# A recommender tower on one core: layer 2 and the MLP one chunk later in TensorE's order of work

## The reference, cut to what matters

```python
# B = 1024 samples, 39 fields, 16 dims; three cross layers of 128 channels each, then an MLP
e = stack([tbl_f[ids[:, f]] for f in range(39)], axis=1)          # 1024 x 39 x 16
xk = e
for W in (f0, f1, f2):                                            # (39*39|128*39|128*39) x 128
    z = einsum('bfd,bgd->bfgd', e, xk).reshape(b, f * g, d)
    xk = einsum('bpd,pm->bmd', z, W);  outs.append(xk)
z = sum(concatenate(outs, axis=1), axis=-1)                       # 1024 x 384
h = concatenate([z, dense_ctx], axis=1)                           # 1024 x 400
h = maximum(h @ W_top1 + b_top1, 0)                               # 512
h = maximum(h @ W_top2 + b_top2, 0)                               # 256
y = h @ W_top3                                                    # 1
```

## Time and profile before

| | |
|---|---|
| median of 3 runs | 1388.26 us (1387.1 to 1389.87) |
| the profiled execution | 1386.06 us |
| its span in the trace | 1383.9 us |
| TensorE busy | 1308.5 us, 95% |
| VectorE, ScalarE, GpSimd busy | 81%, 65%, 51% |
| mean granted TensorE clock | 0.996 |

### The profile page before, as it was taken

How to read it: one execution, slowest core, us unless ns; L and a number is a source line. 1 busy time by engine, 2 the same in 40 slices (tenths; PEclk the granted TensorE clock), 3 DMA queues, 4 the chain that set the end, 5 groups by cost and what they waited for, 6 DMA issues and landing times.

```text
span 1383.9 us, 20103 instructions
## 1 busy us (share of the span) xinstructions
PE 1308.5 (95%) x5912; PEld 997.4 (72%) x5912; DVE 1126.5 (81%) x2794; ACT 905.7 (65%) x3233; POOL 705.0 (51%) x698
## 2 busy tenths in 40 slices
PE   1399999999999999999999999999999999999998
PEld 0356776777777777777777777777777777777787
DVE  2068988888888888888888888888888888888885
ACT  2046776766767676677767667676766777676664
POOL 7786556654545556454566545455564532333200
PEclk9989999999999999999999999999999999999999
DMA  5171021100311012110211003110121102110000
GB/s 138 27 224 47 17 71 50 50 27 3 95 30 43 27 38 68 49 30 14 70 50 50 27 4 95 30 43 28 37 69 50 30 12 68 47 47 26 1 2 0
DMA packets 51172, 63.51 MB, mean 46 GB/s; under 512 B 13067, under 2 KB 24344, under 8 KB 51019
## 3 DMA queue, kind: packets, MB, share of 16 engines
q1 hardware_dynamic: 34544, 56.08, 13.1%
q0 software_dynamic: 10128, 2.98, 2.0%
q10 hardware_dynamic: 6392, 3.18, 0.9%
HBM read 11.08 MB, written 1.02 MB: 9 GB/s over the span
## 4 chain that ended last, share of the span: by engine, by line
PE 77%; DVE 10%; ACT 6%; POOL 3%; issue 3%; DMA 1%; ACTq 0%; DVEq 0%
PE Y L763 17%; PE Y L765 16%; PE Y L764 16%; PE C L711 14%; PE C L725 5%; ACT Y L486 5%; PE S L719 4%; POOL rows L347 3%; DVE sum_a L635 2%; DVE sum_a L630 2%; DVE sum_b L630 2%; DVE z L599 1%; PE C L743 1%; PE S L685 1%; DVE cur L655 1%
## 5 line engine op out<-in xcount | busy, mean ns | idle before, releaser
L486 ACT ACTIVATE Y<-Y,x_col 128x128 f32<-128x128 f32 x2944 | 799.1, 356 | 392.6 <-PE Y L765 379.0
L763 PE MATMUL Y<-f_high,cur_high 128*128 128x512 f32 (+1 forms) x1280 | 626.1, 489 | 10.3 <-DVE part L643 5.0
L764 PE MATMUL Y<-f_low,cur_high 128*128 128x512 f32 (+1 forms) x1280 | 496.2, 388 | 0.0
L765 PE MATMUL Y<-f_high,cur_low 128*128 128x512 f32 (+1 forms) x1280 | 495.9, 387 | 0.0
L385 POOL TENSOR_TENSOR pairs<-shifted,base 117x512 f32<-117x512 f32 x186 | 240.0, 1292 | 462.2 <-PE C L711 460.2
L347 POOL DMA_INDIRECT rows<-in_tbl_dram,ids_sb x312 | 306.8, 983 | 76.8 <-issue 62.9
L763 PEld LDWEIGHTS Y<-f_high,cur_high 128*128 128x128 f32 x1280 | 241.6, 189 | 121.9 <-issue 45.1
L764 PEld LDWEIGHTS Y<-f_low,cur_high 128*128 128x128 f32 x1280 | 242.4, 189 | 89.8 <-issue 52.2
L765 PEld LDWEIGHTS Y<-f_high,cur_low 128*128 128x128 f32 x1280 | 240.9, 188 | 48.6
L630 DVE SCALAR_TENSOR_TENSOR sum_b<-Y,x_col,sum_b 128x128 f32<-128x128 f32 x768 | 262.5, 342 | 0.0
L711 PE MATMUL C<-pairs,f_sum 117*128 117x512 f32 (+1 forms) x448 | 231.5, 599 | 5.2 <-DVE pairs L593 5.2
(11 more groups left out here) (83 smaller groups left out, 660.1 us busy)
## 6 DMA issues: line engine op xcount, KB each, us to landing
shifted<-x_seq SPq DMA_DIRECT2D x157, 234.0 KB
base<-x_seq SPq DMA_DIRECT2D x95, 78.0 KB
rows<-in_tbl_dram,ids_sb POOLq DMA_INDIRECT x312
shifted<-x_seq SPq DMA_DIRECT2D x31, 156.0 KB
G<-in_L_rec_f_dram ACTq DMA_DIRECT2D x3, 832.0 KB, 11.8
w_sb<-in_W_top_dram SPq DMA_DIRECT2D x1, 768.0 KB
f_ext<-in_L_rec_f_dram SPq DMA_DIRECT2D x1, 760.5 KB
w_sb<-in_W_top_dram SPq DMA_DIRECT2D x1, 512.0 KB
```

Source lines behind the costliest of these rows:

```text
L486: ins = act.activation(where[:, i * M:(i + 1) * M], where[:, i * M:(i + 1) * M], ACT.Copy, scale=x_col[:, t // JT % QG, t % JT, f:f + 1])
L763: pe.matmul(where, ch, wh, start=True, stop=False)
L764: pe.matmul(where, ch, wl, start=False, stop=False)
L765: pe.matmul(where, cl, wh, start=False, stop=True).then_inc(y_filled, 1)
```

## The change

Layer 2's four portions are issued at slots 1 to 4 and no longer at 0 to 3 (`AT_L2 = 1`), with the waits that belong to them. The MLP's first layer is issued ahead of chunks 1 and 2 and no longer 0 and 1 (`AT_MLP1 = 1`); its second stays ahead of chunk 5; its last stands ahead of chunk 0 of the next tile and no longer ahead of chunk 9 (`AT_MLP3 = CH`). The chunks, and the programs of the other engines, keep their order.

```diff
 L2_SLICES = [range(0, 4), range(4, 7), range(7, 10), range(10, 13)]
+AT_L2 = 1
+AT_MLP1, AT_MLP2, AT_MLP3 = 1, 5, CH
...
-                    if q and bt and s < len(L2_SLICES):
-                        if s == 0:
+                    if q and bt and AT_L2 <= s < AT_L2 + len(L2_SLICES):
+                        if s == AT_L2:
                             pe.wait_ge(s_read, S_BEFORE["G", TPB * bt - 1] + 1)
                             pe.wait_ge(c_read, C_USE["l2", bt - 1, q - 1])
-                        layer2(bt - 1, [L2_F * (q - 1) + f for f in L2_SLICES[s]], L2_F * (q - 1), L2_F * q)
-                    if mlp is not None and j == mlp_tile(g):
-                        if c == 0:
-                            pe.wait_ge(c_read, C_USE["mlp", mlp, 0])
-                        if c < 2:
-                            mlp1(mlp, (2 * c, 2 * c + 1))
-                        if c == 5:
-                            pe.wait_ge(c_read, C_USE["mlp", mlp, 1])
-                            mlp2(mlp)
-                        if c == 9:
-                            pe.wait_ge(c_read, C_USE["mlp", mlp, 2])
-                            mlp3(mlp)
+                        layer2(bt - 1, [L2_F * (q - 1) + f for f in L2_SLICES[s - AT_L2]], L2_F * (q - 1), L2_F * q)
+                    stage = s - CH * mlp_tile(g) if mlp is not None else None
+                    if stage == AT_MLP1:
+                        pe.wait_ge(c_read, C_USE["mlp", mlp, 0])
+                        mlp1(mlp, (0, 1))
+                    if stage == AT_MLP1 + 1:
+                        mlp1(mlp, (2, 3))
+                    if stage == AT_MLP2:
+                        pe.wait_ge(c_read, C_USE["mlp", mlp, 1])
+                        mlp2(mlp)
+                    if stage == AT_MLP3:
+                        pe.wait_ge(c_read, C_USE["mlp", mlp, 2])
+                        mlp3(mlp)
```

## The result

| | before | after |
|---|---|---|
| median | 1388.42 us (1387.1 to 1389.87, 6 runs) | 1409.85 us (1409.19 to 1411.58, 6 runs) |
| ratio, 95% interval | | 1.0157 (1.0147 to 1.0168) |
| span of the profiled execution | 1383.9 us | 1407.8 us |
| chunk 0 of group 1 to the first matmul of the last chunk | 1242.31 us | 1265.12 us |

The change costs 21.4 us. The exception is group 7, whose last tile was up to 1.4 us longer in some executions (0.2 to 0.6 in four others); where this bears on a reading, the text says so.

The account below looks back on a forecast made before the run. TensorE's stream, busy 95% of the span, was taken as the bound. Uncovered chunk 0 costs 29.6 us, less 2.7 and 1.4 for the MLP's waits: +25.5 us on 1388.26, so 1413.8 us, range 1407 to 1421.

Parts of the forecast that it names:

- the first term: Chunk 0 without cover in 27 groups: 21 starts 1.13 us later and six 0.98 us later, 29.6 us in all.
- Just in time: Group 9 before the change: L643 ended at 436.46 and chunk 0 started at 436.51, read as no delay.
- The second count: Same loss counted from chunk 0 on: 0.10 us later plus 0.93 for four fields behind, 27 x 1.03 = 27.8 us.
- The MLP's first layer: Chunk 0 uncovered in six groups with the MLP in tile 0: 1.13 us later each.
- The MLP's second layer: L743's wait for relu1 on ScalarE goes in seven tiles: 0.38 us each, 2.7 us gained; bounds nothing to 2.7.
- The MLP's last layer: L749's wait for relu2 goes in seven tiles, behind chunk 9: 0.20 us each, 1.4 us gained.
- Covers: Portions at slots 1 to 4 hide the waits of chunks 3 and 4 as before: no gain, no loss.
- the bound: ScalarE's read_y before layer 0's first matmul at slot 12: nothing taken, at most 0.2 us in each of 6 tiles.
- Faster: Rival: chunk 0 is not held by L643, only the named waits matter; 11.5 us saved, 1376.8 us; chance 0.04.
- Given back: Rival: TensorE's longer pause at the start shrinks its later waits in the group equally; 1388 within 3; chance 0.03.
- The clock falls: Rival: each of 27 new pauses lowers TensorE's clock to 1.2 GHz, costing 1.35 us each; 1450 us; chance 0.03.

Follow-up runs that it names:

- the run with the early reads: Kernel before, with ScalarE's and VectorE's reads of layer 0 moved to the very start of the group's last tile: 1377.72 us, ratio 0.9884.
- the reads early: Changed kernel, with ScalarE's and VectorE's reads of layer 0 moved to the very start of the group's last tile: 1381.95 us, ratio 0.9958.
- the later sum: Changed kernel, with VectorE's sum of layer 0 moved behind the reduction of chunks 4 and 5 in a group's last tile: 1401.3 us, ratio 1.0044.

## Why the prediction was right, and where its sizes were off

*Direction and place.* The forecast named the wait that would come (27 new ones, 32 in all, 37 us; found 32 and 38.3 us), the waits that would go, and an unchanged group 1. All four are in the profile after. TensorE's busy time, forecast near 1308 us, is 1302.2. The decisive reading was that of groups 1 to 4 of the kernel before, which already had the order that the change gives to the others.

*Size.* I forecast +25.5 us; it is +21.4 in the medians and +22.81 in the trace. The step that was mis-sized is the first term, 1.13 us for each uncovered chunk 0 with layer 2 in 15 groups and 0.98 in six; it measured 0.97 and 0.96. I counted from the start of the portion, 435.48, as if all of the 1.03 us up to chunk 0 were the portion's own work. It was not. In the stream, where L727 now stands, it takes 0.81 us (442.60 less 441.80 in the rows above; 0.81 by the trace's finer times, in all 21 groups). Of the 0.22 us between them about 0.07 is the slower start behind L725's own wait, and about 0.15 is chunk 0 being held by L643, as the run with the early reads shows. So 1.13 - 0.22 in 15 groups and 0.98 - 0.08 in six, and 0.06 more behind it, mostly at chunk 4, which now follows a portion. "Just in time" for L643's end was the reading that hid this: 0.05 us after the end of the instruction waited for is late, not in time.

The second count, from chunk 0 on, was nearer. Its 0.10 us at chunk 0 is what was measured in all 21 groups, since chunk 0's place already held that wait; the portion behind it cost 0.87 us and not 0.93. Layer 2 alone so makes 20.12 us where the two terms made 15 x 1.13 + 6 x 0.98 = 22.8.

*The MLP's first layer.* 1.13 us in six groups was forecast; 1.15 was measured. The tile in the last group, which I took at nothing, costs 0.16 us. With the gain at the second layer that makes 6 x 1.15 + 0.16 - 7 x 0.47 = 3.8 us, and the run with it alone shows 3.94. Right.

*The MLP's second layer.* 0.38 us in seven tiles was forecast. From chunk 4 to chunk 5 it is 2.78 us after and 3.25 before, 0.47 less. Of that, TensorE's wait for its operand is 0.2 us in the view. Right, and a little low.

*The MLP's last layer.* 0.20 us in seven tiles: the run with it alone shows a gain of 0.30 in all seven, of which 0.21 to 0.23 remain in five and nothing in two. So 1.1 us of the 1.4, with a size for the five that is right by two errors: the wait was worth more, and something behind it was not free. My expectation of 0.3 for that run had the first right and not the second.

Added up: 20.3 + 7.1 - 3.3 - 1.1 = 23.0 us, against 22.81 in the trace. The medians, which hold the start-up as well, differ by 1.4 us less; that rest is not traced to a place.

*Covers.* That portions at slots 1 to 4 would need nothing more is confirmed by the run at slots 2 to 5. That VectorE's read of layer 2 would cost nothing is consistent with the run of layer 2 alone: from group 2 on only the steps into slots 0, 1, 4 and 5 change by more than 0.05 us. For the MLP's last layer the forecast of nothing behind it was wrong by the 0.04 to 0.3 us given above, within the 0.2 us in each of six tiles that I had as the bound except in group 24; whether `read_y` is the cause was not varied.

*The rivals.* "Faster" needed L643 less than 0.15 us behind the group's end. With the reads early, VectorE comes near that (ahead of group 9 L645 ends 0.32 us after the group ahead hands over), and even then the change costs 8.2 us. "Given back": not in the groups with layer 2 or MLP, but this is what happened to the 0.6 us of the later sum in groups 1 to 4. "The clock falls": the windows show 1.00 throughout, and the changed kernel's own first chunk shows 1.00 behind a pause like the one of the earlier trace rows.

## What to carry to other kernels

When a wait is listed at an instruction, look for the next wait that hides behind it before moving the instruction away: work at that place may be covering a longer one. An instruction without a bracket can still be held, if it starts within hundredths of a us of the end of what it needs; a second run or another group in which that ends earlier tells. The cheapest evidence is another stage of the same trace that already has the planned order. And a step that is late on a second engine is better moved on that engine, into its own idle time, than dodged in the order of the engine that waits.

## What the runs showed of the hardware that was not expected

A matmul that starts behind a wait delays the next one by 0.07 to 0.08 us, and about as much for a small matmul as for a large one. A 128-column fp32 pass is followed after 0.18 us behind L725's wait and after 0.11 us in the stream; the first 512-column matmul of chunk 0 is followed after 0.30 us behind its wait (120.23 to 120.53 in group 1) and after 0.23 us in the stream. A whole chunk 0 behind its wait so takes 0.77 us, against 0.69 for a bare chunk.

From the end of VectorE's L645 to the start of the chunk 0 that waits for it the changed kernel shows 0.14 to 0.15 us at all 31 starts, with TensorE idle ahead of it for 0.8 to 1.6 us. Where TensorE had been busy until just before, with a portion of layer 2 in the kernel before, it was 0.05 to 0.06 us.
